# First self attention of a six-stage decoder kernel: the probabilities are scaled by their row sums before they are turned

## The reference, cut to what matters

```
q, k, v = x @ Wq + bq, x @ Wk + bk, x @ Wv + bv        (heads of 64 features)
weights = softmax(q k^T / sqrt(8))                     (512 x 512 a head)
feats   = weights @ v                                  (512 x 512 in all heads)
return feats @ Wo + bo
```

## Time and profile before

| | |
|---|---|
| median of 3 runs | 2902.24 us (2897.63 to 2905.83) |
| span of the profiled execution, first to last instruction | 2871.8 us |
| own time of the profiled execution | not listed; the median lies 30.4 us above its span |
| PE busy | 2673.5 us, 93% of the span |
| DVE busy | 1806.2 us, 63% |
| ACT busy | 1420.3 us, 49% |
| POOL busy | 294.5 us, 10% |
| first self attention | from 0 to about 465 us of the span |

### The profile page before, as it was taken

One profiled execution on the slowest core, in us unless ns is written; L12 is line 12 of the kernel. 1 busy time (PEld: TensorE's weight loads), 2 busy tenths in 40 slices (PEclk: granted clock), 3 DMA queues, 4 the chain that ended last, 5 costly groups with the idle time before them and its releaser, 6 DMA issues. The chain is left out here.

```text
span 2871.8 us, 40570 instructions
## 1 busy us (share of the span) xinstructions
PE 2673.5 (93%) x12750; PEld 1685.2 (59%) x12750; DVE 1806.2 (63%) x3475; ACT 1420.3 (49%) x2978; POOL 294.5 (10%) x399
## 2 busy tenths in 40 slices
PE   8999997979999987999999999997999999997898
PEld 4555554444588863677777777775545455443444
DVE  5666674654543326756755756754777777775676
ACT  4454463322133322554553653743577676664665
POOL 1230003001711114000000000001110101000000
PEclk9999998989999999999999999998899999999999
DMA  3395105541687754323223223211000000001000
GB/s 140 86 123 143 58 15 184 186 141 54 200 277 234 248 184 148 115 103 109 73 106 110 68 104 124 66 67 59 5 6 6 5 2 5 2 2 71 26 23 30
DMA packets 114169, 266.30 MB, mean 93 GB/s; under 512 B 14464, under 2 KB 37008, under 8 KB 113200
## 3 DMA queue, kind: packets, MB, share of 16 engines
q1 hardware_dynamic: 97152, 211.16, 22.2%
q0 software_dynamic: 16816, 52.64, 7.8%
HBM read 208.97 MB, written 58.48 MB: 93 GB/s over the span
## 5 line engine op out<-in xcount | busy, mean ns | idle before, releaser
L2506 DVE TENSOR_REDUCE x_neg_max<-bank 128x1 f32<-128x512 f32 x512 | 327.1, 684 | 99.7 <-PE bank L2351 99.2
L2458 ACT ACTIVATE x_weights<-bank 128x512 f32<-128x512 f32 x512 | 279.1, 599 | 127.8 <-PE bank L2362 122.9
L1885 ACT ACTIVATE a_probs<-bank,a_neg_max 128x128 f32<-128x128 f32 (+3 forms) x256 | 136.1, 532 | 206.0 <-DVE a_neg_max L1979 202.0
L1785 PE MATMUL bank<-a_x_high,a_weights 128*128 128x512 f32 x640 | 218.3, 404 | 8.2 <-DMA a_weights<-split_qkv 2.3
L109 PEld LDWEIGHTS bank<-all_ident,a_probs 128*128 128x128 f32 x1200 | 151.5, 140 | 85.0 <-issue 47.0
L109 PE MATMUL bank<-all_ident,a_probs 128*128 128x128 f32 x1200 | 193.3, 273 | 3.0 <-ACT a_probs_t L1877 2.2
L1877 ACT COPY a_probs_t<-bank 128x128 f32<-128x128 f32 (+3 forms) x256 | 107.6, 420 | 144.2 <-PE bank L109 143.8
L1820 PE MATMUL bank<-a_k_cols,a_q_cols 128*128 128x128 f32 (+3 forms) x512 | 176.7, 434 | 0.4 <-DVE a_q_cols L1928 0.2
L1849 PE MATMUL bank<-a_wo,a_att_high 128*128 128x512 f32 x512 | 162.1, 398 | 3.9 <-DVE a_q_cols L1928 2.9
L1510 DVE TENSOR_TENSOR moe_acc<-bank,moe_acc 128x512 f32 x79 | 54.6, 692 | 171.1 <-PE bank L1176 170.5
L1165 PE MATMUL bank<-moe_gh_cols,moe_item 128*128 128x256 f32 x632 | 151.8, 383 | 3.0 <-DMA moe_item<-moe_items 2.7
(11 more groups left out here) (413 smaller groups left out, 5437.0 us busy)
## 6 DMA issues: line engine op xcount, KB each, us to landing
a_weights<-split_qkv SPq DMA_DIRECT2D x80, 512.0 KB, 3.6
moe_item<-moe_items SPq DMA_DIRECT2D x79, 257.0 KB, 3.8
moe_item<-moe_items SPq DMA_DIRECT2D x79, 256.0 KB, 3.7
a_wo<-split_out SPq DMA_DIRECT2D x8, 2048.0 KB, 7.8
a_wo<-split_out SPq DMA_DIRECT2D x16, 1024.0 KB, 9.9
split_qkv<-x_qkv_parts SPq DMA_DIRECT2D x12, 1024.0 KB, 5.1
moe_items<-in_L_ffn_e_w POOLq DMA_DIRECT2D x40, 256.0 KB
split_out<-a_turned SPq DMA_DIRECT2D x8, 1024.0 KB, 4.0
```

The lines of the kernel that those rows point to most:

```text
L1785: last = pe.matmul(mm[g % 2], weight[:, k, :], x[:, k, :], start=n == 0, stop=n == 3 * KD - 1)
L1885: act.activation(probs[:, n % SLOTS, 0:t], sc[n % 4][:, 0:t], ACT.Exp, bias=neg_max[:, n:n + 1], accum_out=row_sum[:, n:n + 1]).then_inc(s ...
L2458: act.activation(weights[:, chunk % 2, k, :], weight_banks[slot % 2], ACT.Exp).then_inc(s.weight.free, 1)
L2506: dve.tensor_reduce(neg_max[:, g % 2, j, h:h + 1], score_banks[slot % 3], AX.X, ALU.max, negate=True) \
```

## The change

Probabilities of tile n are now divided by their row sum right behind the exponential, in SBUF, before PE turns them. For an even tile DVE takes the reciprocal and multiplies the 128 x 512 tile (at DVE's step n+1). For an odd tile DVE takes the reciprocal only, and ACT multiplies (an ACTIVATE of the function Copy with a scale, at ACT's step n+1, between the exponential and the copy out of `ta`). PE's turn waits for the scaled tile (`even_ready`, `odd_ready`) and no longer for the exponential. The product of a group is then finished and already lies features x tokens, as the output projection needs it: ACT copies it as the high part at its steps 20 and 28, and for group 2 at step 36 (`keep_feats`), DVE subtracts for the low part at steps 21, 29 and 37 (`low_feats`), and both treat the last group behind the loop. Gone are `products`, `feats`, the turns back of lines 303 and 307, and the copies around them. The output projection waits for the low part of the last group. DVE adds the bias rows before that.

```
-    COPY_LAG, BACK_LAG, FEATS_LAG = 12, 14, 15
+    FEATS_LAG = 13
-    Q0, SC = NT, TILES + 2 * NT
-    TA, TV, MM = TILES // 2, TILES // 2, 3 * KD + 2 * GROUPS + NT
+    Q0, SC = NT, TILES + NT
+    TA, TV, MM = TILES // 2, TILES // 2, 3 * KD + GROUPS + NT
...
-        feats_high, feats_low = q_parts[:, 0:KD, :], q_parts[:, KD:2 * KD, :]
-        feats = sb("feats", [P, NT, D])
+        feats_high, feats_low = q_parts[:, 0:GROUPS, :], sb("feats_low", [P, GROUPS, S], F32R)
...   (PE, in the loop)
-                        pe.wait_ge(s.sc.free, b * SC + s.sc.size + Q0 + n + 1)
                         if n % 2 == 0:
+                            pe.wait_ge(s.even_ready, b * TA + n // 2 + 1)
                             pe.wait_ge(s.ta.free, b * TA + n // 2 + 1)
                             turn_tile(pe, ta[0], probs[:, n % SLOTS, :], m.ident[:], NT).then_inc(s.ta.full, 1)
                         else:
+                            pe.wait_ge(s.odd_ready, b * TV + n // 2 + 1)
...
-                    g, at = divmod(i - BACK_LAG - (GT - 1), GT)
-                    if at == 0 and 0 <= g < GROUPS:
-                        n = 3 * KD + 2 * g + 1
-                        pe.wait_ge(s.mm.free, b * MM + s.mm.size + n)
-                        turn_tile(pe, mm[n % 2], products[:], m.ident[:], NT).then_inc(s.mm.full, 1)
-                pe.wait_ge(s.mm.free, b * MM + s.mm.size + 3 * KD + 2 * GROUPS)
-                for j in range(NT):
-                    pe.wait_ge(s.sc.free, b * SC + F0 + j + 1)
-                    turn_tile(pe, sc[j], feats[:, j, :], m.ident[:], KD).then_inc(s.sc.full, 1)
...
+                    pe.wait_ge(s.mm.free, b * MM + s.mm.size + 3 * KD + GROUPS)
...   (ACT)
+                def keep_feats(g):
+                    n = 3 * KD + g
+                    act.wait_ge(s.mm.full, b * MM + n + 1)
+                    act.copy(feats_high[:, g, :], mm[n % 2]).then_inc(s.feats_high_ready, 1)
...
+                    if 0 < i <= TILES and i % 2 == 0:
+                        n = i - 1
+                        act.wait_ge(s.inv_ready, b * TV + n // 2 + 1)
+                        act.activation(probs[:, n % SLOTS, :], probs[:, n % SLOTS, :], ACT.Copy, scale=inv_sum[:, n:n + 1]).then_inc(s.odd_ready, 1)
...   (behind the copy out of ta)
+                    g, at = divmod(i - FEATS_LAG - (GT - 1), GT)
+                    if at == 0 and 0 <= g < GROUPS - 1:
+                        keep_feats(g)
+                keep_feats(GROUPS - 1)
...   (DVE)
+                def low_feats(g):
+                    n = 3 * KD + g
+                    dve.wait_ge(s.feats_high_ready, b * GROUPS + g + 1)
+                    dve.tensor_tensor(feats_low[:, g, :], mm[n % 2], feats_high[:, g, :].bitcast(F32), ALU.subtract).then_inc(s.mm.free, 1)
...
+                    if 0 < i <= TILES:
+                        n = i - 1
+                        dve.wait_ge(s.sc.free, b * SC + s.sc.size + Q0 + n + 1)
+                        inverse = dve.reciprocal(inv_sum[:, n:n + 1], row_sum[:, n:n + 1])
+                        if n % 2 == 0:
+                            dve.drain()
+                            dve.tensor_scalar(probs[:, n % SLOTS, :], probs[:, n % SLOTS, :], inv_sum[:, n:n + 1], None, ALU.mult).then_inc(s.even_ready, 1)
+                        else:
+                            inverse.then_inc(s.inv_ready, 1)
...   (behind the copy out of tv)
+                    g, at = divmod(i - FEATS_LAG - GT, GT)
+                    if at == 0 and 0 <= g < GROUPS - 1:
+                        low_feats(g)
...
-                bias_rows(0, 2)
-                for j in range(NT):
-                    tile = slice(j * P, (j + 1) * P)
-                    dve.wait_ge(s.feats_high_ready, b * NT + j + 1)
-                    dve.tensor_tensor(feats_low[:, :, tile], blocks_of(sc[j], KD), feats_high[:, :, tile].bitcast(F32),
-                                      ALU.subtract).then_inc(s.sc.free, 1)
-                bias_rows(2, NT)
+                bias_rows(0, NT)
+                low_feats(GROUPS - 1)
```

More of the change, by code:

```diff
@@ L166, in self_attention_0 @@
         neg_max, row_sum, inv_sum = sb("neg_max", [P, TILES]), sb("row_sum", [P, TILES]), sb("inv_sum", [P, TILES])
-        probs, products = sb("probs", [P, SLOTS, S]), sb("products", [P, S])
+        probs = sb("probs", [P, SLOTS, S])
         turned = [sb(f"turned_{i}", [P, NT, S]) for i in range(TURNED - 2)] + [x_rows, x_cols]
@@ L261, in batch @@
                 pe.wait_ge(s.low_done, b * PARTS + PARTS)
-                for i in range(TILES + FEATS_LAG + 1):
+                for i in range(TILES + FEATS_LAG):
                     if i < TILES:
@@ L282, in batch @@
                         c = PACE.index(at)
-                        n = 3 * KD + 2 * g
+                        n = 3 * KD + g
                         if c == 0:
@@ L345, in batch @@
                     last.then_inc(s.high_done, 1)
-                for i in range(TILES + TA_LAG):
+                for i in range(TILES + FEATS_LAG):
                     if i < TILES:
@@ L420, in _ @@
                         if j == 1 and h >= TURNED:
-                            dve.wait_ge(s.mm.full, b * MM + 3 * KD + 2 * ((h - TURNED + 1) // GROUP) + 1)
+                            dve.wait_ge(s.mm.full, b * MM + 3 * KD + (h - TURNED + 1) // GROUP + 1)
                         dve.tensor_copy(turned[buffer_of(h)][:, :, j * P:(j + 1) * P], blocks_of(tv[0], NT)).then_inc(s.tv.free, 1)
-                    g, at = divmod(i - COPY_LAG - (GT - 1), GT)
-                    if at == 0 and 0 <= g < GROUPS:
-                        n = 3 * KD + 2 * g
-                        dve.wait_ge(s.mm.full, b * MM + n + 1)
-                        dve.tensor_copy(products[:], mm[n % 2]).then_inc(s.mm.free, 1)
-                    g, at = divmod(i - FEATS_LAG - (GT - 1), GT)
-                    if at == 0 and 0 <= g < GROUPS:
-                        n = 3 * KD + 2 * g + 1
-                        sums = slice(g * GT, (g + 1) * GT)
-                        dve.wait_ge(s.mm.full, b * MM + n + 1)
-                        dve.reciprocal(inv_sum[:, sums], row_sum[:, sums])
-                        dve.drain()
-                        dve.tensor_tensor(feats[:, :, g * P:(g + 1) * P].rearrange("p j (h d) -> p j h d", h=GROUP),
-                                          mm[n % 2].rearrange("p (j h d) -> p j h d", j=NT, h=GROUP),
-                                          inv_sum[:, sums].rearrange("p (h j) -> p j h", h=GROUP).unsqueeze(3).to_broadcast([P, NT, GROUP, HD]),
-                                          ALU.mult).then_inc(s.mm.free, 1)
-                first = 3 * KD + 2 * GROUPS
+                    g, at = divmod(i - FEATS_LAG - GT, GT)
+                    if at == 0 and 0 <= g < GROUPS - 1:
+                        low_feats(g)
+                first = 3 * KD + GROUPS
                 dve.wait_ge(w_out, 32)
```

15 lines of the change are left out of this document (5 added, 10 removed).

## The result

The changed kernel takes 2919.61 us (median of 5 runs, 2915.06 to 2921.41) against 2902.24 for the kernel before: a ratio of 1.0056 with a 95% interval of 1.0042 to 1.0070, so 16 us or 0.56% slower. I had forecast 2909 with a range of 2887 to 2925. The sign and most of the mechanism were right; the size was not, and part of the agreement is luck: the costs that I had not seen (about 16 us) were larger than the whole sum that I had (7 us), and one batch in four hardly counts. The most likely outcome by my chances was less than 0.3% from no change; the kernel is slower than that, and by my own case, to which I gave 0.08 for such an outcome.

A forecast was written before the change was run, and what follows sets the result against it. PE, busy for 93% of the span, was taken as the limit, with DVE full at each batch's head. Terms of +5.1 + 2.2 - 5.2 us a batch, 8.4 in four, less 1.3, gave +7: 2909 us, range 2887 to 2925.

The forecast's parts named there:

- my own case: First self attention: PE's savings are about offset by waits for DVE; +7 us, 2909 us in all, chance 0.48.
- The chain: Behind each batch's last product: one ACT copy and one DVE subtraction remain, 1.42 us; saves 3.2, in the second batch 4.5.
- The head of the batch: Steps 0 to 12, before products: DVE's added scaling makes two tiles take 2.77 us instead of 1.80; 5.1 us lost a batch.
- The steps of the high part: ACT's steps 20 and 28: PE's odd turns come 0.6 and 1.6 us late; 2.2 us lost a batch.
- (a) to (c): Removed product turns, group 3's wait for group 2's copy, and the shorter end chain: 5.2 us saved a batch, 22.1 in all.
- SP and POOL keep their queues: Whole change: no DMA is moved and the instruction queues of SP and POOL stay; no cost was entered.
- my +2.1 a batch: Net per batch of the first self attention: +5.1 + 2.2 - 5.2 us, counted for four batches.
- Rival A: First stretch of each batch: PE's clock falls to the lower level, about 4 us a batch, 2925 us; chance 0.20.
- the two signs by which I said I would be wrong: Second batch's first product 14 us or less after its first maximum, or that stretch's granted clock leaving 1.00.
- Rival B: Head of the batch: scaling is hidden because DVE and ACT run ahead; 2880 us, half hidden 2890; chance 0.18.
- Rival C: Stretch with products: DVE becomes the limit, two tiles take 3.3 us instead of 3.0; +11 us, 2920 us; chance 0.14.
- My own sign for this stretch: From step 14 on: two tiles at 3.0 us, with ACT's wait for PE's turns nearly gone.

The follow-up runs named there:

- the earlier trace: The trace of the unchanged kernel before from which the forecast was made; its span was 2871.8 us.
- the second trace: The kernel before, unchanged, traced again; it took 2901.84 us with a span of 2900.1.
- the mended order: Changed kernel with ACT's high part before its `ta` copy, DVE's `tv` copy before reciprocal and multiplication, and POOL's weight split beside the value projections; ratio 1.0001.

## Why the prediction was right or wrong

**The chain** was right. It was to take 1.42 us and takes 1.49, for 4.63 in the earlier trace rows. The extra 1.3 us of the second batch's longer chain belonged to one execution: the granted clock was 0.75 there, and in the second trace, at 1.00, the second batch's chain takes 4.64 us like the others. DVE's bias rows were over by 237.1 us, three before they could have been in the way.

**The head of the batch** was right in mechanism, short in size: 2.77 us a pair to the hundredth, the last maximum of it 15.69 us after the first (15.7 forecast), but +5.7 a batch instead of +5.1. The step that failed put the product right behind DVE's copy of tile 7. Between them stands PE's turn of tile 9, which needs the same single bank and starts only after that copy: 0.56 us.

**The steps of the high part** were right in place and sign: waits at tiles 21 and 29, forecast 0.6 and 1.6 us, measured 1.27 and 2.17. I had followed the path through ACT's scaling. The path that ended last goes through DVE, which waits for the high part ahead of its own copy out of `tv`; that is why the first wait is there without scaling too (1.28), and why the move of one ACT instruction removes it. Without ACT's multiplication both waits stay (1.27 and 2.19), so ACT's scaling is not on that path; moving DVE's copy ahead removes the first as well. My term (a) to (c) of 22 us is in part for the same reason only 15 net in the kernel without scaling: 1.3 us of new wait in each batch stand against it. Its size was right: the first, third and last batch are 3.9, 3.6 and 4.1 us shorter there than in the second trace, with the 1.3 us back 5.2, 4.9 and 5.4, for my 5.2.

**The first batch** was missed: +4.3 us more. The step that failed is "SP and POOL keep their queues", read as if POOL then cost nothing. POOL's instructions didn't move, but DVE's work beside them changed its kind, from reading PSUM (six maxima beside POOL take 3.91 us in the first batch of the second trace, and 3.90 without POOL in the earlier trace rows) to SBUF on both sides.

**The count of batches** was wrong: I multiplied by four. The second batch's period is set in good part by POOL's queue and late transfers, so it can take up what its own work adds or saves. With my +2.1 a batch this is small; with the true +4 to +10 it hides about a quarter.

**Rival A** (the clock) was half right. In the first stretch of the second, third and last batch, where I had put it, the clock stayed at 1.00, with PE busy for 3.46 of 5 us in the second:

```profile
188.00:193.00 5.00, 3.46 (x24) 2.68 (x23) 4.55 (x12) 4.54 (x13) 0.00 (x0) 1.00 1.02 96
```

It fell behind the long waits instead: after POOL's hold in the first batch, and after tile 29 in three batches, 1.4 to 1.65 us each. The fall in the first batch lies in the first stretch, so one of the two signs by which I said I would be wrong did come there, for a reason (POOL's hold) that neither my case nor A had. **Rival B** (hidden scaling) is refuted: the scaling costs 31 us. **Rival C** shows only faintly: pairs with products take 3.0 and 3.2 us in turn (195.01, 198.03, 201.22 for the starts of the quarters), 0.1 over the forecast on average and not the 0.3 that it asked for. My own sign for this stretch, that ACT's wait for PE's turns would be nearly gone, did not come either: 0.46 to 0.90 us, for 0.93 in the earlier trace rows.

The sum of +7 had thus errors of both signs. It missed 2.4 us at the heads, 4.3 in the first batch, 5 at the two stalls and some 4.5 of clock, about 16 in all, and some 0.7 a batch for the pairs at 3.1 us. Against it stands a second batch whose share can't be read from the traces. The third batch closes: +2.1 forecast, and the 0.6, 1.2, 1.6 and 0.7 us that were missed give the +6.2 of the table. And the forecast was set against a trace that was quick in the second batch.

## What to carry to other kernels

When work is moved from behind a loop into it, look for the stretch where the engine that gets it has no idle time, and for what stands behind it in that engine's queue: the same instructions at another place in the step were worth 0.25 to 0.4% here. A stretch paced by other engines than PE is a place to put PE's independent work; together with the mended order that turned this change from 0.56% slower to 0.43% faster. And before multiplying by the number of repetitions, check from two traces that each repetition is bound by the same thing.

## What I had not expected of the hardware

- DVE's multiplication in SBUF of a 128 x 512 float32 tile was held until a POOL instruction beside it ended: 3.00 us for 0.49. Four subtractions with both inputs in SBUF took 7.06 us for 2.78. Maxima out of PSUM and additions with one input in PSUM kept their durations.
- The same wait of PE was followed by a fall of the granted clock in one kernel's first three batches and not in another's (46.1 against 44.5 us for the stretch).
- POOL issued a transfer 1.02 us after the last of sixty transfers that it had issued before had landed, 70 to 79 us after POOL was otherwise ready, and the arithmetic behind it on POOL came later still.
- Beside those sixty transfers a load of 512 KB took 37.6 us to land, for 6.4 and 6.8 without them.
